# Where the first tile is turned, and where the scatters sit: a gated cross-attention and expert kernel on one core

## Chip, core and metric

One NeuronCore of one Trainium2 chip. The metric is the device time of one execution in microseconds (us). Engine names in the profile: PE is TensorE, PEld its weight loads, DVE VectorE, ACT ScalarE, POOL GpSimd, SP the engine whose queue (SPq) issues most DMAs.

## The reference, cut to what matters

```python
# 16 batches of 128 tokens, width 128; ctx of width 256; 8 heads of 16
x = x + tanh(g_xattn) * xattn(ctx, layernorm(x), mask, mask, ...)
#   k, v from ctx; q from layernorm(x); masked softmax; out = W_out [tgt, update] + b_out
x = x + tanh(g_ffn) * ffn(layernorm(x))
def ffn(x):                                    # 2048 tokens, 9 experts, hidden 352
    scores = sigmoid(x @ gate.T + bias)
    top_scores, selected = top_k(scores, 2)    # normalised to sum 1
    for e in range(9):
        h = silu(x @ w1[e].T) * (x @ w3[e].T)
        out += cw[:, e:e+1] * (h @ w2[e].T)
```

Each token goes to two experts. The kernel writes every token's normalised row twice into a table in HBM (`x_rows`), ordered by expert, and works through that table in 40 tiles of 128 rows. A tile holds the rows of one expert only.

## The kernel before, in words

Every engine runs its own instruction list in the order of the program; semaphores tie the lists together. An engine that waits for a semaphore holds up all that is behind it in its list.

**Projections** (the first 33 us) make keys, queries and values of all batches.

**Attention steps.** `turns(step)` runs step k = 0 to 16 on all engines. In step k, batch k gets its scores (PE), maxima (DVE, L850) and exponentials (ACT, L412); batch k-1 is transposed and multiplied with the values; batch k-2 is turned back, divided (DVE `unturn`, `upd`, L860), multiplied with W_out (PE `gate_and_out`, L1304) and added to x (DVE `second`, L890 to L896, which also takes mean and variance); batch k-3 is normalised (DVE `norm2`, L869, into `stage`), turned (PE `turn_rows`, L1294) and gated (L1302). The 1/sqrt of the variance is taken on POOL: `rstd2_of(b)` (L586 `ve`, L588 `rs`). `norm2(b)` waits for it, and `turn_rows` waits for `norm2`. So in step k the chain is: `second(k-3)` in step k-1, POOL `rstd2_of(k-3)`, DVE `norm2(k-3)`, PE `turn_rows(k)`.

**Routing.** Batches go in four groups of four. When a group's gate logits are there, DVE clamps them, takes the sigmoid (with exponentials from ACT), finds the top two (`find_top`), marks them (`mark_top`), PE ranks them (`rank`, L1257 to L1261), and DVE works out weights and target rows (`weigh`, `keep_ranks`, `place_rows`, `label_rows` with L844). The labels of group g = 0 and 1 are ready at the end of steps 8 and 12, those of group 2 at the end of step 16.

**Scatters.** POOL writes the rows with indirect DMAs (`scatter`, L616), two per batch. Groups 0 and 1 together are 16 pieces, `piece(0)` to `piece(15)`; pieces 0 to 7 are group 0, pieces 8 to 15 group 1. `ROWS` says which piece is issued in which step: a tuple for early (behind `rstd2_of`) and one for late (behind `keep`, the copy of the normalised row). `scatter` of group g first waits for `label_set` g+1. Group 2 is scattered behind the attention steps, group 3 behind the result of tile 1.

**Tables.** `table_counts(n)` (= `count_tiles` and `pass_tiles`) and `table_rows(n)` on DVE work out which rows and which expert each tile has: n = 0 for tiles 0 to 7, n = 1 for 8 to 15, n = 2 for the rest. `table_used` says what is consumed. The loads of tiles 0 to 7 (SP, L319) wait for the landing of all scatters of groups 0 and 1; those of tiles 8 to 15 for group 2's; the rest for group 3's.

**Tiles.** `tile_turns(tile, between)` runs step k = 0 to 42; I call them tile steps. In tile step k PE turns tile k (L1353), makes the two hidden products of tile k-1 (`hidden`, L1342 to L1344, six matmuls), the output of tile k-3 (L1384) and the transposes of tile k-2 (L1393), in this order. ACT splits off the high part of the turned tile (L466), takes the Silu (L473) and copies; DVE makes the low part (`xg_low`, L1066), the product of the gates (`hid`, L1074) and casts an id (L1023). POOL scatters each result to `y_rows` (L643).

The last batch's and last group's chain is laid into the first tile steps: `gate_and_out(17)`, `second(15)`, `norm2(15)`, `turn_rows(18)`, `gate_and_out(18)`, then the routing of group 3. One tile step, `SWITCH`, is special: ACT there loads the table of Exp and that of Silu again (L495, L497), and DVE does ACT's three copies of that step in its place (L1029, L1034, L1039).

At the end PE adds up the last two tiles with one-hot matrices (L1430), the sums come back from `y_rows`, and the output is stored.

Of the kernel before, what the change touches and what calls it, by code (L numbers as in the profile page):

```python
# [59 lines left out]
SWITCH = 3  # L60
VALUES = {0: (0,), 1: (1,), 2: (2,), 3: (3,), 4: (4, 5), 5: (6, 7), 6: (8, 9), 7: (10, 11, 12), 8: (13, 14, 15)}
ROWS = {9: ((0,), (1,)), 10: ((2,), (3,)), 11: ((4,), (5,)), 12: ((6,), (7,)), 13: ((8,), (9,)), 14: ((10,), (11,)), 15: ((12,), (13,)), 16: ((14, 15), ())}
# [8 lines left out]
def build(nc, x, ctxT, mask, first, consts, row_consts, w_srcT, w_tgtT, w_outT, w13T, w2T, gateT, x_rows, y_rows, out):  # L71
    with ExitStack() as ctx:
# [163 lines left out]
        def has(k, lag):  # L236

            return 0 <= k - lag < NT
# [109 lines left out]
        def _(act):  # L348
# [109 lines left out]
            nc.scalar.preload_act_table(ACT.Silu)  # L458
            turned_back(NB + 1)

            def tile(k, r, i):
                if has(k, 0) and not in_switch(k):
                    act.wait_ge(x_turned, k + 1)
                    if k >= 2:
                        act.wait_ge(h3_mm, k - 1)
                    nc.scalar.copy(xg_high[:, r % 2, :], bank[6][:, 0:P]).then_inc(x_high, 1)  # L466
# [197 lines left out]
        def _(dve):  # L664
# [332 lines left out]
            table_used(0)  # L997
            table_counts(1)
# [42 lines left out]
            def within(k):  # L1041

                if k == SWITCH:
                    table_rows(1)
                    result_in_switch(k - 3)
                    turned_in_switch(k - 2)
                    add_one(NG - 1)
                if k == 4:
                    above_knee(NG - 1)
                if k == 5:  # L1050
                    mark_top(NG - 1)
                if k == 6:
                    keep_ranks(NG - 1)
                    place_rows(NG - 1)
                    label_rows(NG - 1)
                if k == 9:
                    table_rows(2)
# [31 lines left out]
            def between(k):  # L1089

                if k == 0:
                    second(NB - 1)
                if k == 1:
                    norm2(NB - 1)
                if k == SWITCH - 1:
                    logits_of(NG - 1)
                    clamp(NG - 1)
                if k == 4:
                    find_top(NG - 1)
                if k == 5:  # L1100
                    weigh(NG - 1)
                if k == 6:
                    table_used(1)
                if k == 7:
                    count_tiles(2)
                if k == 8:
                    pass_tiles(2)
# [25 lines left out]
        def _(pe):  # L1133
# [162 lines left out]

            def gate_and_out(k):

                pe.wait_ge(ul_copied, k - 1)
                if on(k, 3):  # L1300
                    at = 3 * P + (k - 3) % UN * NE
                    nc.tensor.matmul(ps_b[:, at:at + NE], ulT[:, k % 2, 1, :], gate_w[:], start=True, stop=True).then_inc(lg_mm, 1)  # L1302
                if on(k, 2):
                    nc.tensor.matmul(ps_b[:, 2 * P:3 * P], ulT[:, k % 2, 0, :], w_outg[:, 1, :], start=True, stop=True).then_inc(o_mm, 1)  # L1304
# [11 lines left out]
            keep_busy(0, 5)  # L1316
            turn_rows(NB + 1)
# [30 lines left out]
            def tile(k, r, i):  # L1348
                if has(k, 0):
                    pe.wait_ge(ld_tile[r], i * 16 + 16)  # L1350
                    if k >= 1:
                        pe.wait_ge(x_low, k)
                    nc.tensor.transpose(bank[6][:, 0:P], xg[:, r, 0:D], ident).then_inc(x_turned, 1)  # L1353
                if in_switch(k):
                    gate_and_out(NB + 2)
                if has(k, 1):
# [6 lines left out]
                    hidden(bank[2 + q], q, e, 1).then_inc(h3_mm, 1)  # L1363
                if has(k, 0):
# [36 lines left out]
            def between(k):  # L1401

                if k == 0:
                    gate_and_out(NB + 1)
                if k == 5:
                    rank(NG - 1)
# [99 lines left out]
```

## Time and profile before

| what | value |
|---|---|
| median of 3 runs | 213.8 us (213.61 to 214.6) |
| the profiled execution | 213.55 us, of which the span 211.8 us |
| PE, DVE, ACT, POOL busy | 201.5, 146.2, 141.5, 128.3 us |
| granted TensorE clock | 1.00 throughout |
| DMA | 34.91 MB, mean 165 GB/s |

The span runs from the first to the last instruction. In a timeline row the columns are: start and length in us, engine, line, operation, tiles written and read, count, and in brackets how long the engine had been idle and what released it. Starts are more telling than lengths, since the pipelined engines overlap successive instructions.

### The profile page before, as it was taken

The page shows a single profiled execution, that of the slowest core. Times are in us where ns is not written, and L with a number is a line of the kernel's source. Part 1 is how long each engine was busy: PE and PEld are TensorE (multiplying, and loading weights), DVE is VectorE, ACT ScalarE, POOL GpSimd, SP SyncE. Part 2 cuts the span into 40 slices and gives each one's busy share as a digit, 9 for nine tenths or more (in the row PEclk, how much of TensorE's full clock was granted, in tenths as well). Part 3 has the DMA queues.
Part 4 walks back from the last instruction along what each step waited for, and adds up shares of the span by engine and source line. Part 5 has one row for each costly group of instructions (what it writes and reads, how often), then busy time and mean ns, then how long its engine had stood idle before and what let it go on. Part 6 is the DMA issues. An engine that isn't in the chain of part 4 may idle for free.

```text
span 211.8 us, 5793 instructions
## 1 busy us (share of the span) xinstructions
PE 201.5 (95%) x1608; PEld 162.7 (77%) x1608; DVE 146.2 (69%) x523; ACT 141.5 (67%) x398; POOL 128.3 (61%) x231
## 2 busy tenths in 40 slices
PE   8999998999999999999979899999999999999993
PEld 3686575567666676666648789999999999999893
DVE  0369979787889968899987997544343434456674
ACT  2365896999886788588846766766667676666200
POOL 5227655027664686567767867788888856567200
PEclk9999999999999999999999999999999999999999
DMA  5999999999993011000015923422322222270196
GB/s 144 379 365 264 390 408 406 393 392 324 329 354 101 7 35 39 27 26 27 28 52 107 256 64 99 83 85 69 87 69 70 58 62 53 63 246 29 37 346 223
DMA packets 23601, 34.91 MB, mean 165 GB/s; under 512 B 2561, under 2 KB 15878, under 8 KB 23442
## 3 DMA queue, kind: packets, MB, share of 16 engines
q1 hardware_dynamic: 20610, 29.27, 42.6%
q0 software_dynamic: 2240, 4.23, 6.2%
q10 hardware_dynamic: 720, 1.02, 1.6%
q8 instruction: 15, 0.25, 0.5%
q14 instruction: 16, 0.13, 0.2%
HBM read 15.85 MB, written 19.06 MB: 165 GB/s over the span
## 4 chain that ended last, share of the span: by engine, by line
PE 65%; DVE 15%; ACT 5%; issue 5%; DMA 4%; POOL 4%; SPq 1%; POOLq 0%; DVEq 0%; ACTq 0%
PE pt_ps L1384 10%; PE score_ps L1342 5%; PE pt_ps L1393 5%; PE score_ps L1197 5%; PE score_ps L1344 5%; PE score_ps L1343 5%; PE pt_ps L1235 4%; PE ps_a L1247 3%; PE pt_ps L1137 3%; DMA kheads<-y_rows 3%; PE score_ps L1147 3%; DVE less L850 2%; ACT probs L412 2%; PE ps_a L1353 2%; POOL y_rows L643 2%
## 5 line engine op out<-in xcount | busy, mean ns | idle before, releaser
L643 POOL DMA_INDIRECT y_rows<-vals,ids x38 | 37.7, 992 | 14.2 <-ACT vals L484 7.9
L412 ACT ACTIVATE probs<-score_ps,less 128x128 f32<-128x128 f32 x128 | 37.5, 406 | 1.7 <-DVE less L850 1.7
L616 POOL DMA_INDIRECT x_rows<-stage,slot x32 | 32.6, 1018 | 9.1 <-issue 7.7
L1384 PE MATMUL pt_ps<-w,probsT 128*128 x234 | 32.6, 275 | 0.9 <-DVE probsT L1039 0.6
L1384 PEld LDWEIGHTS pt_ps<-w,probsT 128*128 128x128 f32 x234 | 30.8, 191 | 1.6 <-issue 1.4
L1066 DVE TENSOR_TENSOR xg_low<-ps_a,xg_high 128x128 fp32r<-128x128 f32 x40 | 11.6, 290 | 29.2 <-ACT xg_high L466 28.8
L484 ACT ACTIVATE vals<-pt_ps,xg 128x128 f32<-128x128 f32 x38 | 13.9, 367 | 26.6 <-PE pt_ps L1384 26.6
L1342 PE MATMUL score_ps<-w_high,xg_low 128*128 x80 | 29.2, 364 | 0.0
L1344 PE MATMUL score_ps<-w_high,xg_high 128*128 x80 | 25.9, 323 | 0.0
L1343 PE MATMUL score_ps<-w_low,xg_high 128*128 x80 | 25.6, 320 | 0.0
L1074 DVE TENSOR_TENSOR probs<-probs,score_ps 128x352 f32<-128x352 f32 x40 | 20.8, 520 | 6.1 <-ACT probs L473 2.7
L850 DVE TENSOR_REDUCE less<-score_ps 128x4 f32<-128x512 f32 x32 | 21.7, 684 | 3.5 <-PE score_ps L1204 3.4
L473 ACT ACTIVATE probs<-score_ps 128x352 f32<-128x352 f32 x40 | 18.6, 464 | 1.3 <-PE score_ps L1344 1.2
L1393 PE MATMUL pt_ps<-fst,probs 128*128 128x128 f32 x117 | 19.2, 273 | 0.1
L491 ACT COPY probsT<-pt_ps 128x384 f32<-128x384 f32 x38 | 18.2, 478 | 0.3 <-PE pt_ps L1393 0.2
L1197 PE MATMUL score_ps<-kheads,qT 64*128 64x256 f32 x128 | 18.2, 402 | 0.2
L1235 PE MATMUL pt_ps<-fst,probs 128*128 128x128 f32 x128 | 17.1, 274 | 1.0 <-ACT probs L412 1.0
L586 POOL TENSOR_SCALAR ve<-mv 128x1 f32<-128x1 f32 x16 | 3.6, 227 | 20.3 <-DVE mv L896 20.3
L1235 PEld LDWEIGHTS pt_ps<-fst,probs 128*128 128x128 f32 x128 | 14.4, 141 | 2.0 <-ACT probs L412 1.9
L1342 PEld LDWEIGHTS score_ps<-w_high,xg_low 128*128 128x128 f32 x80 | 15.1, 189 | 0.5 <-issue 0.2
L1343 PEld LDWEIGHTS score_ps<-w_low,xg_high 128*128 128x128 f32 x80 | 15.2, 190 | 0.0
L1344 PEld LDWEIGHTS score_ps<-w_high,xg_high 128*128 128x128 f32 x80 | 15.0, 188 | 0.0
(184 smaller groups left out, 442.8 us busy)
## 6 DMA issues: line engine op xcount, KB each, us to landing
x_rows<-pads SPq DMA_DIRECT2D x1, 9945.0 KB, 37.7
w_low<-in_w13T SPq DMA_DIRECT2D x3, 1056.0 KB, 11.5
xg<-x_rows SPq DMA_DIRECT2D x40, 65.0 KB, 2.0
ctx_r<-in_ctxT SPq DMA_DIRECT2D x4, 512.0 KB, 7.5
y_rows<-pads SPq DMA_DIRECT2D x1, 2048.0 KB, 18.7
w<-in_w2T SPq DMA_DIRECT2D x1, 1728.0 KB, 13.2
kheads<-y_rows SPq DMA_DIRECT2D x3, 512.0 KB, 5.0
mask_b<-in_mask SPq DMA_DIRECT2D x4, 256.0 KB, 8.2
```

Of the source, the lines that this page charges most:

```text
L412: last = nc.scalar.activation(probs[:, r % 2, h, :], score_ps[:, r % 2, h, :], ACT.Exp, bias=less[:, r % 2, h:h + 1])
L616: pool.indirect_dma_start(x_rows[:, :], bass.IndirectOffsetOnAxis(ap=slot[:, par, c, p:p + 1], axis=0), stage[:, par, c, p, :], None, boun ...
L643: pool.indirect_dma_start(y_rows[:, :], bass.IndirectOffsetOnAxis(ap=ids[:, s:s + 1], axis=0), yt[:, s, :], None, bounds_check=last_row, o ...
L850: nc.vector.tensor_reduce(less[:, r % 2, here], score_ps[:, r % 2, here, :], AX.X, ALU.max, negate=True).then_inc(lessened, 1)
L1074: nc.vector.tensor_tensor(hid[:, q, :], gated[:, q, :], bank[2 + q][:, 0:HID], ALU.mult).then_inc(hid_done, 1)
L1197: nc.tensor.matmul(score_ps[:, r % 2, half * HH + 2 * pair:half * HH + 2 * pair + 2, :], qT[rows, k * P:(k + 1) * P], kheads[rows, heads, ...
L1235: last = nc.tensor.transpose(pt_ps[:, half, h, :], probs[:, q, half * UN + h, :], ident)
L1342: nc.tensor.matmul(dst[:, 0:HID], xg_low[:, q, :], of(w13_high), start=True, stop=False)
L1343: nc.tensor.matmul(dst[:, 0:HID], xg_high[:, q, :], of(w13_low), start=False, stop=False)
L1344: return nc.tensor.matmul(dst[:, 0:HID], xg_high[:, q, :], of(w13_high), start=False, stop=True)
L1384: last = nc.tensor.matmul(into[:, 0:D], hidT[:, q3, c, :], w2[:, bass.ds(e3, 1), c, :].rearrange("p o d -> p (o d)"), start=(c == 0), stop ...
L1393: last = nc.tensor.transpose(bank[4][:, c * P:(c + 1) * P], hid[:, q2, c0:c0 + P], ident)
```

## The change

What it does, by engine:

- PE: tile 0 is turned behind the filler matmuls (`keep_busy(0, 5)`) and ahead of `turn_rows(17)`; `gate_and_out(17)` moves from behind tile step 0 into tile step 1, behind `hidden` of tile 0; `turn_rows(18)` and `gate_and_out(18)` come one tile step later; so does `rank(3)`.
- ACT: the high part of tile 0 is taken ahead of `turned_back(17)`.
- `SWITCH` goes from 3 to 4, and with it the Exp and Silu tables and the switched copies.
- DVE: `table_used(0)` and `table_counts(1)` leave the place ahead of tile 0. `table_used(0)` goes to tile step 0, `count_tiles(1)` to 2, `pass_tiles(1)` to 3; `table_rows(1)` stays in the switch step and goes behind the two switched copies. `second(15)` moves from behind tile step 0 to inside tile step 1 (ahead of `hid`), `norm2(15)` one step later, all of group 3's routing one step later, `add_one` out of the switch step.
- POOL: `piece(2)` is issued in step 9 rather than 10, and so every second piece a place sooner: step 9 has three pieces, step 16 one. `piece(8)`, the first of group 1, goes from early in step 13 to late in step 12, and `piece(15)` from second to first in step 16.

```diff
-SWITCH = 3
+SWITCH = 4
-ROWS = {9: ((0,), (1,)), 10: ((2,), (3,)), 11: ((4,), (5,)), 12: ((6,), (7,)), 13: ((8,), (9,)), 14: ((10,), (11,)), 15: ((12,), (13,)), 16: ((14, 15), ())}
+ROWS = {9: ((0,), (1, 2)), 10: ((3,), (4,)), 11: ((5,), (6,)), 12: ((7,), (8,)), 13: ((9,), (10,)), 14: ((11,), (12,)), 15: ((13,), (14,)), 16: ((15,), ())}
@@ scalar
+            def high_rows(k, r):
+                act.wait_ge(x_turned, k + 1)
+                if k >= 2:
+                    act.wait_ge(h3_mm, k - 1)
+                nc.scalar.copy(xg_high[:, r % 2, :], bank[6][:, 0:P]).then_inc(x_high, 1)
+            high_rows(0, 0)
             turned_back(NB + 1)
             def tile(k, r, i):
-                if has(k, 0) and not in_switch(k):
+                if has(k, 0) and k >= 1 and not in_switch(k):
+                    high_rows(k, r)
@@ vector
             norm2(NB - 2)
-            table_used(0)
-            table_counts(1)
             def within(k):
+                if k == 0:
+                    table_used(0)
+                if k == 1:
+                    second(NB - 1)
+                if k == 2:
+                    count_tiles(1)
+                if k == SWITCH - 1:
+                    pass_tiles(1)
                 if k == SWITCH:
-                    table_rows(1)
                     result_in_switch(k - 3)
                     turned_in_switch(k - 2)
+                    table_rows(1)
+                if k == 5:
                     add_one(NG - 1)
-                if k == 4:
                     above_knee(NG - 1)
-                if k == 5:
+                if k == 6:
                     mark_top(NG - 1)
...
             def between(k):
-                if k == 0:
-                    second(NB - 1)
-                if k == 1:
+                if k == 2:
                     norm2(NB - 1)
...
@@ tensor
+            def turn_tile(k, r, i):
+                pe.wait_ge(ld_tile[r], i * 16 + 16)
+                if k >= 1:
+                    pe.wait_ge(x_low, k)
+                nc.tensor.transpose(bank[6][:, 0:P], xg[:, r, 0:D], ident).then_inc(x_turned, 1)
             keep_busy(0, 5)
+            turn_tile(0, 0, 0)
             turn_rows(NB + 1)
             def tile(k, r, i):
...
                     hidden(bank[2 + q], q, e, 1).then_inc(h3_mm, 1)
+                if k == 1:
+                    gate_and_out(NB + 1)
             def between(k):
-                if k == 0:
-                    gate_and_out(NB + 1)
-                if k == 5:
+                if k == 6:
                     rank(NG - 1)
```

Left out are the remaining steps of the routing in `within` and `between`, all one tile step later (`keep_ranks` to `label_rows` 7, `table_rows(2)` 10, `find_top` 5, `weigh` 6, `table_used(1)` 7, `count_tiles(2)` 8, `pass_tiles(2)` 9).

## Rows read from the trace of the kernel before

**Rows 1.** The page: busy time of the engines, and the last chain's shares.

```profile
PE 201.5 (95%) x1608; PEld 162.7 (77%) x1608; DVE 146.2 (69%) x523; ACT 141.5 (67%) x398; POOL 128.3 (61%) x231
...
PE 65%; DVE 15%; ACT 5%; issue 5%; DMA 4%; POOL 4%; SPq 1%; POOLq 0%; DVEq 0%; ACTq 0%
```

**Rows 2.** Stretches: length, busy time of each engine, clock, DMA share, GB/s.

```profile
110.00:137.00 27.00, 25.14 (x183) 23.14 (x184) 21.74 (x105) 17.36 (x45) 20.61 (x29) 1.00 0.50 123
137.00:197.00 60.00, 59.67 (x464) 59.44 (x463) 28.36 (x93) 39.91 (x116) 45.33 (x91) 1.00 0.29 80
```

**Rows 3.** Timeline of POOL: steps 9 and 10, and the scatters of group 3.

```profile
74.58 0.98 POOL L616 DMA_INDIRECT x_rows<-stage,slot  x1 [0.17 <-issue]
75.59 0.24 POOL L586 TENSOR_SCALAR ve<-mv 128x1 f32<-128x1 f32 x1
75.92 0.57 POOL L588 TENSOR_TENSOR rs<-ve,minus_half 128x1 f32<-128x1 f32 x1
...
126.24 0.99 POOL L616 DMA_INDIRECT x_rows<-stage,slot  x1 [1.43 <-DVE slot L844]
127.54 0.97 POOL L616 DMA_INDIRECT x_rows<-stage,slot  x1 [0.30 <-issue]
```

**Rows 4.** Timeline of DVE: `norm2` of step 10, labels of group 1, `norm2` of step 13.

```profile
76.82 0.34 DVE L869 SCALAR_TENSOR_TENSOR stage<-xs,mv,rs 128x128 f32<-128x128 f32 x1
...
90.52 0.20 DVE L844 CAST slot<-slot_f 128x8 int32<-128x8 f32 x1
...
91.67 0.34 DVE L869 SCALAR_TENSOR_TENSOR stage<-xs,mv,rs 128x128 f32<-128x128 f32 x1
```

**Rows 5.** Timeline of PE: the turned row of steps 10 and 13.

```profile
77.22 0.33 PE L1294 MATMUL ps_b<-fst,stage 128*128 128x128 f32 x1
...
92.07 0.33 PE L1294 MATMUL ps_b<-fst,stage 128*128 128x128 f32 x1
```

**Rows 6.** Timeline of POOL: pieces 14 and 15 in step 16.

```profile
104.67 1.09 POOL L616 DMA_INDIRECT x_rows<-stage,slot  x1 [0.19 <-issue]
106.07 0.97 POOL L616 DMA_INDIRECT x_rows<-stage,slot  x1 [0.30 <-issue]
```

**Rows 7.** Timeline of PE: fillers, tile 0, `gate_and_out(17)`, `hidden`, tiles 6 to 8.

```profile
108.37 1.24 PE L1267 MATMUL score_ps<-ones 128*128 128x512 bf16 x5
...
110.88 0.33 PE L1353 MATMUL ps_a<-fst,xg 128*128 128x128 f32 x1 [0.61 <-DMA xg<-x_rows]
...
111.19 0.47 PE L1304 MATMUL ps_b<-w_outg,ulT 128*128 128x128 f32 x2
...
112.24 0.42 PE L1342 MATMUL score_ps<-w_high,xg_low 128*128 x1
...
113.37 0.42 PE L1342 MATMUL score_ps<-w_high,xg_low 128*128 x1
...
123.53 0.31 PE L1353 MATMUL ps_a<-fst,xg 128*128 128x128 f32 x1
...
125.83 0.27 PE L1353 MATMUL ps_a<-fst,xg 128*128 128x128 f32 x1
...
127.89 0.27 PE L1353 MATMUL ps_a<-fst,xg 128*128 128x128 f32 x1
```

**Rows 8.** Timeline of DVE: `count_tiles(1)`, `xg_low` 0, `second(15)`, `hid` 0, `mark_top(3)`.

```profile
110.18 0.16 DVE L955 TENSOR_SCALAR in_tiles<-placed 1x9 f32<-1x9 f32 x1
...
111.62 0.29 DVE L1066 TENSOR_TENSOR xg_low<-ps_a,xg_high 128x128 fp32r<-128x128 f32 x1
111.83 0.28 DVE L890 TENSOR_TENSOR xs<-ps_b,xs 128x128 f32<-128x128 f32 x1
...
113.57 0.52 DVE L1074 TENSOR_TENSOR probs<-probs,score_ps 128x352 f32<-128x352 f32 x1 [0.58 <-ACT probs L473]
...
122.79 0.22 DVE L799 TENSOR_TENSOR choices<-cst,top_at 128x72 f32<-128x72 f32 x1
```

**Rows 9.** Timeline of POOL: the result scatter of tile 24.

```profile
170.33 0.99 POOL L643 DMA_INDIRECT y_rows<-vals,ids  x1 [0.60 <-POOL ids L633]
```

More of the change, by code:

```diff
@@ L458, in _ @@
             nc.scalar.preload_act_table(ACT.Silu)
+            def high_rows(k, r):
[4 more added lines that the diff above has]
+            high_rows(0, 0)
             turned_back(NB + 1)
             def tile(k, r, i):
-                if has(k, 0) and not in_switch(k):
[L463 to L466, printed above, removed]
+                if has(k, 0) and k >= 1 and not in_switch(k):
+                    high_rows(k, r)
                 if has(k, 1):
@@ L1041, in within @@
             def within(k):
+                if k == 0:
[6 more added lines that the diff above has]
+                    pass_tiles(1)
                 if k == SWITCH:
-                    table_rows(1)
                     result_in_switch(k - 3)
                     turned_in_switch(k - 2)
+                    table_rows(1)
+                if k == 5:
                     add_one(NG - 1)
-                if k == 4:
                     above_knee(NG - 1)
-                if k == 5:
+                if k == 6:
                     mark_top(NG - 1)
-                if k == 6:
+                if k == 7:
                     keep_ranks(NG - 1)
@@ L1055, in within @@
                     label_rows(NG - 1)
-                if k == 9:
+                if k == 10:
                     table_rows(2)
@@ L1097, in between @@
                     clamp(NG - 1)
-                if k == 4:
+                if k == 5:
                     find_top(NG - 1)
-                if k == 5:
+                if k == 6:
                     weigh(NG - 1)
-                if k == 6:
+                if k == 7:
                     table_used(1)
-                if k == 7:
+                if k == 8:
                     count_tiles(2)
-                if k == 8:
+                if k == 9:
                     pass_tiles(2)
@@ L1348, in tile @@
             def tile(k, r, i):
[L1349 to L1353, printed above, removed]
+                if has(k, 0) and k >= 1:
+                    turn_tile(k, r, i)
                 if in_switch(k):
@@ L1401, in between @@
             def between(k):
-                if k == 0:
-                    gate_and_out(NB + 1)
-                if k == 5:
+                if k == 6:
                     rank(NG - 1)
```

## The prediction

> **What bounds the kernel now.** I read the page first: PE is busy 95% of the span and carries 65% of the chain that ended last, DVE 15%, POOL only 4% [rows 1]. The small shares matter, because the stretches differ. From 137 to 197 us PE is busy 59.67 of 60 us: nothing but PE's own work sets the pace there, and tile follows tile every 2.06 us (125.83 to 127.89) [rows 2, 7]. From 110 to 137 it is busy 25.14 of 27 us while DVE is busy 21.74 and POOL 20.61 [rows 2]: here PE waits, mostly for DVE. The change touches this junction, and through POOL the attention steps 9 to 16. So the questions are: when does PE reach tile 7 or 8 at full pace, and does a POOL instruction of an attention step come on the path. I then went through the timelines of POOL, DVE and PE.
>
> **POOL, step 9: one more scatter.** POOL works in order. In step 9 the late scatter starts at 74.58 and takes 0.98; `ve` of step 10 starts at 75.59, right at its end, and `rs` ends at 75.92 + 0.57 = 76.49 [rows 3]. DVE's `norm2` started at 76.82, so 0.33 was to spare, of which 0.03 is the release [rows 4]. Now two late scatters stand there. The second costs a gap of 0.30 and 0.98, as in the pair at 126.24 and 127.54 (1.30 from start to start) [rows 3]: 1.28. `rs` ends at 77.77, `norm2` starts at 77.80, 0.98 late; PE's L1294, 0.40 behind `norm2` before (77.22) [rows 5], comes 0.98 late. All of PE's step is behind it in its list, ACT's exponentials are behind the copy of what it turns, and the second maxima behind `norm2` on DVE. PE is the longest of the three in these steps, so nothing gives the time back. Bounds: 0 (a scatter that holds nothing up) and 1.3 (all of it on the path); the rows lie at 0.98, and I take that.
>
> The Trainium skill speaks against this. "DMA: Bandwidth & Descriptors", section "Anatomy of one DMA — SWDGE (gpsimd) path", counts descriptor generation as small and says that many descriptors can be emitted before the added cost shows. The trace disagrees for this indirect form: 0.98 us, with the next POOL instruction right at the end. By the rule this term would be 0, and the next one would lose 0.98; that is a rival below.
>
> **POOL, step 12: piece 8 waits for labels.** Piece 8 belongs to group 1, whose labels DVE finishes at 90.52 + 0.20 = 90.72, at the very end of its step 12 [rows 4]. Before, it was issued in step 13, behind `rstd2_of(10)`. Now it stands late in step 12 and POOL stops on it, with `rstd2_of(10)` queued behind. It starts some 0.28 after the label (the released one at 126.24 shows a wait of this kind) [rows 3], at 91.00, ends at 91.98; `ve` and `rs` take 0.90 (75.59 to 76.49), to 92.88; `norm2(10)` starts at 92.91, not 91.67 [rows 4]. PE's L1294 of step 13 follows at 93.31, not 92.07 [rows 5]: 1.24 late, and again all is behind it. It had no slack at all: `norm2` began when `upd` left DVE. Bounds: 0, if POOL could pass the waiting scatter, and 1.4 with the longest scatter, 1.09 [rows 6]; I take 1.24. In the other steps each piece only changes its name, not its place in time, and costs 0.
>
> **POOL, step 16: piece 15 lands sooner.** From its start (106.07) to PE's turn of tile 0 (110.88, released by the load) it took 4.81 us [rows 6, 7]. It now starts at 104.67 and is 0.12 longer: tile 0 is ready at 109.60. SP has nothing else ahead of these loads. The fillers end at 108.37 + 1.24 = 109.61 [rows 7], so the turn at 109.63 waits for nothing and costs PE nothing, since `turn_rows(17)` behind it waits for `norm2(14)` till 109.9 anyway. If the landing were later, `turn_rows(17)` would be late by as much.
>
> **The junction on PE and DVE.** (Times of the clock before; 2.22 are to be added.) From the turn of tile 0 to `hidden` of it the chain took 112.24 - 110.88 = 1.36 [rows 7]. From 109.63 that gives 110.99: a lead of 1.25. What is next late is `hid` 0 on DVE. `second(15)` stands ahead of it and needs `gate_and_out(17)`, now behind the six matmuls of `hidden` (1.06 of the 1.13 from 112.24 to 113.37), so W_out's product starts at 110.99 + 1.06 + 0.24 and takes 0.47 [rows 7]: 112.76. The add starts at about 112.8, and the three instructions of `second` take 0.86 with their waits; `hid` 0 starts at 113.6 or so. Before it started at 113.57 [rows 8]. The lead has gone into DVE's waiting: DVE has only `table_used(0)` (0.38) to do meanwhile, where before it did the table counts.
>
> From `hid` 0 to `mark_top(3)` DVE took 122.79 - 113.57 = 9.22 [rows 8], nearly without a pause. To it come `count_tiles(1)` and `pass_tiles(1)`, which stood ahead of tile 0: 111.62 - 110.18 = 1.44 [rows 8], and the DVE work of one tile more (0.21 + 0.44 + 0.06 = 0.71, from start to start), and about 0.1 for waits on the gate logits and on the output in the switch step: 11.5. `mark_top(3)` starts at about 125.05. PE's `rank(3)` is released by it and now stands ahead of tile 7, not of tile 6. Before, the turn behind it came 123.53 - 122.79 = 0.74 behind `mark_top` [rows 7, 8], so tile 7 is turned at 125.79 against 125.83, and tile 8, by the 2.30 of that step, at 128.09 against 127.89 [rows 7]: 0.20 late. From there all is as before. Putting `table_rows(1)` behind the switched copies saves PE a wait at the output matmuls, but the DVE work stays, and it ends in the wait at `rank`. Bounds of this term: -2.9, if PE never waited from tile 1 to tile 7 (its own work there is 12.1 us by the spacing of its rows, from 110.8 on), and +1.3, if each moved item waits once more; the rows that decide are DVE's, so I take +0.20.
>
> **The end.** Labels of group 3 come about 2.3 later, relative to this clock, so POOL's eight scatters and behind them the result scatters start 2.3 late, 2.1 against PE. At tile 24 POOL had just caught up: that scatter waited 0.60 for its own id, not for a result [rows 9]. Its own spacing there is 0.99 + 0.03 + 0.20 + 0.60 = 1.82 against PE's 2.06, so 2.1 us of arrears take 9 tiles, till tile 33 of 38. It is just hidden: 0.
>
> **The sum.** 0.98 + 1.24 + 0.20 = 2.42. The profiled execution took 213.55 us (span 211.8), the changed one 215.97; the median of the runs shown is 213.8, 0.25 above the profiled one, so I forecast 216.2, 1.1% slower.
>
> **The rivals.**
> - *The lead is kept.* DVE's waits turn out shorter and PE keeps the 1.25 at tile 7, with both POOL delays: 213.8 + 2.22 - 1.25 = 214.8. For it: DVE has pauses in the early tile steps into which work may fit. Against: the 11.5 us of DVE work ahead of `rank`.
> - *Cheap scatters* (the skill's rule): posting takes POOL next to nothing. Step 9 costs 0, step 12 only the wait, 1.24 - 0.98 = 0.26, the junction 0.20: 214.3. Against: [rows 3].
> - *The other side, faster: the junction's waits go.* The lead and the copies ahead of `table_rows(1)` take out every wait of PE up to tile 7: -2.9, against +2.22: 213.1; below that if a POOL delay is smaller. Its place is `rank(3)`, and it decides if `mark_top(3)` starts before PE is ready for it, about 122.2 on the clock before. Against: DVE would have to do 11.5 us of work in 8.6.
> - *The end shows.* If POOL's arrears are a microsecond larger than I reckon, or DVE's late one-hot rows slow POOL, the last result scatter, and the sum behind it, come up to 1 us later: 217.2. For it: tile 24 without slack [rows 9].
>
> **How the numbers follow.** Forecast 0.55, lead kept 0.13, cheap scatters 0.08, faster side 0.10, the end 0.14. The forecast alone has 215.4 to 216.9. The range goes from 214.0, which takes in the cheap scatters and the kept lead, to 217.8 with the end; the faster side and a tenth of the rest lie outside. About 0.5% (1.07 us) is what a measurement can tell from no change: slower beyond it are forecast and end, 0.69; within it the two middle cases, 0.21; faster 0.10.
>
> **What would show it.** In the changed profile: L616 late in step 12 with an idle time of about 3 us released by DVE `slot`; L1294 of steps 10 and 13 each released by `stage`, with PE idle about 1 us; the turn of tile 0 right behind the fillers; `hid` 0 no sooner behind the fillers than now; PE idle about 1 us ahead of `rank`; `y_rows` scatters waiting for ACT again at the end. I am wrong if POOL's `ve` starts before the scatter ahead of it has ended, or if tile 8 is turned less than 19 us behind the fillers' start (before: 19.5).

## The result, and the profile after

| | before | after |
|---|---|---|
| median (runs) | 213.87 us (4) | 217.22 us (4; 216.65 to 217.65) |
| ratio after/before, 95% interval | | 1.0143 (1.0115 to 1.0171) |
| profiled execution, span | 213.55, 211.8 | 217.65, 215.9 |

The change makes the kernel slower: by 3.35 us between the medians, by 1.4% in the ratio on record. The forecast was 216.2 with a range up to 217.8: the sign, both POOL delays and the range hold; the sum is 1.0 too small.

**A common clock first.** The spans differ by 4.1, not 3.3. The rest is older than the change: the row of batch 5 that PE turns in step 8, ahead of every edit, stands 0.76 later in the profiled execution of after. That is the start-up: in the fourteen kernels of this document, which are the same up to there, the row stands anywhere from 67.86 to 69.26. So all marks below are counted from the start of that row. First before, then after, PE's timeline:

```profile
68.12 0.27 PE L1294 MATMUL ps_b<-fst,stage 128*128 128x128 f32 x1
```

```profile
68.88 0.27 PE L1304 MATMUL ps_b<-fst,stage 128*128 128x128 f32 x1
```

| mark, us from that row | before | after | later by | forecast |
|---|---|---|---|---|
| `turn_rows(17)` on PE | 41.82 | 44.09 | 2.27 | 2.22 |
| tile 0 turned | 42.76 | 43.61 | 0.85 | 0.97 |
| `hid` 0 starts on DVE | 45.45 | 47.59 | 2.14 | 2.25 |
| `mark_top(3)` starts on DVE | 54.67 | 60.12 | 5.45 | 4.48 |
| tile 7 turned | 57.71 | 60.84 | 3.13 | 2.18 |
| tile 8 turned | 59.77 | 63.24 | 3.47 | 2.42 |
| tile 13 turned | 70.31 | 73.60 | 3.29 | 2.42 |

(The forecast's times of the clock before, plus the 2.22.) All is as forecast down to `hid` 0, and the microsecond is lost between there and `mark_top(3)`.

The page of after (line numbers have moved: L1304 was L1294, L622 was L616, L592 and L594 were L586 and L588). POOL's share of the chain has risen from 4% to 7%, PE's has fallen from 65% to 62% [rows 1]; the scatter group says whom POOL waits for:

```profile
PE 202.2 (94%) x1608; PEld 163.1 (76%) x1608; DVE 146.4 (68%) x523; ACT 141.7 (66%) x398; POOL 128.7 (60%) x231
...
PE 62%; DVE 15%; POOL 7%; issue 5%; ACT 5%; DMA 4%; SPq 1%; POOLq 0%; ACTq 0%; DVEq 0%
...
L622 POOL DMA_INDIRECT x_rows<-stage,slot x32 | 32.9, 1027 | 14.5 <-DVE slot L850 7.3
```

Stretches of after, columns as in [rows 2], laid 3 us later. The tiles' stretch is PE's alone as before; at the junction PE is busy 23.89 of 27 us where it was 25.14 [rows 2]:

```profile
113.00:140.00 27.00, 23.89 (x174) 22.01 (x175) 21.34 (x105) 16.30 (x42) 18.09 (x25) 1.00 0.42 107
140.00:199.00 59.00, 59.00 (x459) 58.98 (x459) 27.32 (x92) 39.68 (x115) 46.62 (x92) 1.00 0.30 84
```

**The two POOL delays.** POOL's timeline of after, steps 9 and 10, then 12 and 13:

```profile
75.34 0.98 POOL L622 DMA_INDIRECT x_rows<-stage,slot  x1 [0.17 <-issue]
76.63 0.97 POOL L622 DMA_INDIRECT x_rows<-stage,slot  x1 [0.30 <-issue]
77.62 0.25 POOL L592 TENSOR_SCALAR ve<-mv 128x1 f32<-128x1 f32 x1
...
92.66 0.98 POOL L622 DMA_INDIRECT x_rows<-stage,slot  x1 [3.59 <-DVE slot L850]
93.66 0.25 POOL L592 TENSOR_SCALAR ve<-mv 128x1 f32<-128x1 f32 x1
```

In step 9 the second late scatter starts 1.29 behind the first, and `ve` stands right at its end. In step 12 piece 8 stops POOL for 3.59 us on the labels (3 forecast), with `ve` and `rs` of batch 10 behind it, which `norm2(10)` needs. PE's timeline shows what follows, where both rows had no idle time ahead of them before [rows 5]:

```profile
78.97 0.33 PE L1304 MATMUL ps_b<-fst,stage 128*128 128x128 f32 x1 [0.91 <-DVE stage L875]
...
95.00 0.33 PE L1304 MATMUL ps_b<-fst,stage 128*128 128x128 f32 x1 [1.21 <-DVE stage L875]
```

From row to row step 10 grows from 4.30 to 5.29 (+0.99; forecast 0.98), step 13 from 4.43 to 5.68 (+1.25; forecast 1.24). Step 14 grows by 0.11 and step 11 gives 0.07 back; neither was in the sum.

**The junction.** PE's timeline of after, answering to [rows 7]: tile 0 right behind the fillers, the W_out product of batch 15 behind the six of `hidden` 0, row 18, tiles 6, 7 and 8:

```profile
111.42 1.24 PE L1277 MATMUL score_ps<-ones 128*128 128x512 bf16 x5
112.49 0.27 PE L1312 MATMUL ps_a<-fst,xg 128*128 128x128 f32 x1
...
114.01 0.42 PE L1360 MATMUL score_ps<-w_high,xg_low 128*128 x1
...
115.21 0.47 PE L1321 MATMUL ps_b<-w_outg,ulT 128*128 128x128 f32 x2
...
119.26 0.30 PE L1304 MATMUL ps_b<-fst,stage 128*128 128x128 f32 x1 [0.34 <-issue]
...
125.40 0.55 PE L1410 MATMUL pt_ps<-fst,probs 128*128 128x128 f32 x3 [0.72 <-DVE probs L1086]
125.78 0.27 PE L1312 MATMUL ps_a<-fst,xg 128*128 128x128 f32 x1
...
129.51 0.19 PE L1267 MATMUL ps_b<-both,rows_below 128*128 128x36 bf16 x1 [1.13 <-DVE both L811]
...
129.72 0.31 PE L1312 MATMUL ps_a<-fst,xg 128*128 128x128 f32 x1
...
132.12 0.27 PE L1312 MATMUL ps_a<-fst,xg 128*128 128x128 f32 x1
```

DVE's timeline of after, answering to [rows 8]: `second(15)`, `hid` 0, the gate logits, the first copy of the switch step, `over` of the routing, `mark_top(3)`:

```profile
115.71 0.29 DVE L896 TENSOR_TENSOR xs<-ps_b,xs 128x128 f32<-128x128 f32 x1 [0.89 <-PE ps_b L1321]
...
116.47 0.50 DVE L1086 TENSOR_TENSOR probs<-probs,score_ps 128x352 f32<-128x352 f32 x1
...
120.91 0.20 DVE L881 TENSOR_TENSOR z<-ps_b,cst 128x36 f32<-128x36 f32 x1 [0.84 <-PE ps_b L1319]
...
122.65 0.35 DVE L1038 TENSOR_SCALAR vals<-pt_ps,xg 128x128 f32<-128x128 f32 x1 [0.59 <-PE pt_ps L1401]
...
126.25 0.67 DVE L783 TENSOR_SCALAR over<-sigs 128x36 f32<-128x36 f32 x1
...
129.00 0.22 DVE L805 TENSOR_TENSOR choices<-cst,top_at 128x72 f32<-128x72 f32 x1
```

PE stands 1.13 us ahead of `rank(3)`, as forecast; but it also lost 0.72 a step earlier to DVE's `hid`. From `hid` 0 to `mark_top(3)` DVE took 129.00 - 116.47 = 12.53 us, not 11.5. It stood still for the gate logits (0.84) and for the output (0.59), 1.43 together; before, these two instructions waited 0.24 and nothing. And L783 took 0.67 instead of 0.35. I had put 0.1 for all of this. Two instructions went the other way: from start to start `key` (L770, before L764) took 0.21 instead of 0.42, and the cast of the packed experts (L987, before L981) 0.10 instead of 0.27, together 0.38 less.

### The profile page after: what moved, and what is told of

It reads as the page before. It is cut to its first block, busy times and chain, and to the rows that moved or that the text cites. A ratio compares the mean times of both kernels' runs of the same rounds, so it can differ in the third digit from the quotient of the medians.

```text
span 215.9 us, 5792 instructions
## 1 busy us (share of the span) xinstructions
PE 202.2 (94%) x1608; PEld 163.1 (76%) x1608; DVE 146.4 (68%) x523; ACT 141.7 (66%) x398; POOL 128.7 (60%) x231
## 3 DMA queue, kind: packets, MB, share of 16 engines
q10 hardware_dynamic: 720, 1.02, 1.6%
## 4 chain that ended last, share of the span: by engine, by line
PE 62%; DVE 15%; POOL 7%; issue 5%; ACT 5%; DMA 4%; SPq 1%; POOLq 0%; ACTq 0%; DVEq 0%
PE pt_ps L1401 10%; PE score_ps L1360 5%; PE score_ps L1362 5%; PE score_ps L1361 5%; PE pt_ps L1410 5%; PE score_ps L1207 4%; PE pt_ps L1147 4%; PE pt_ps L1245 3%; DMA kheads<-y_rows 3%; PE ps_a L1257 3%; PE score_ps L1157 2%; ACT probs L412 2%; DVE less L856 2%; PE ps_a L1312 2%; POOL y_rows L649 2%
## 5 line engine op out<-in xcount | busy, mean ns | idle before, releaser
L622 POOL DMA_INDIRECT x_rows<-stage,slot x32 | 32.9, 1027 | 14.5 <-DVE slot L850 7.3
L1245 PEld LDWEIGHTS pt_ps<-fst,probs 128*128 128x128 f32 x128 | 14.4, 141 | 2.0 <-ACT probs L412 1.9
L592 POOL TENSOR_SCALAR ve<-mv 128x1 f32<-128x1 f32 x16 | 3.7, 229 | 20.0 <-DVE mv L902 20.0
L1410 PEld LDWEIGHTS pt_ps<-fst,probs 128*128 128x128 f32 x117 | 14.0, 141 | 1.5 <-DVE probs L1086 1.5
```

Of the source, the lines that this page charges most:

```text
L622: pool.indirect_dma_start(x_rows[:, :], bass.IndirectOffsetOnAxis(ap=slot[:, par, c, p:p + 1], axis=0), stage[:, par, c, p, :], None, boun ...
L1245: last = nc.tensor.transpose(pt_ps[:, half, h, :], probs[:, q, half * UN + h, :], ident)
L1410: last = nc.tensor.transpose(bank[4][:, c * P:(c + 1) * P], hid[:, q2, c0:c0 + P], ident)
```

## The experiments

What was open: whether the two delays are caused by the pieces' places alone, and which edit of the tile phase costs the rest. `ROWS` of before, of after, and three others. PE marks as above, "later" against before; "step 10" and "step 13" are the change of the distance between two turned rows:

| kernel | ratio to before (95%) | step 10 | step 13 | `turn_rows(17)` later | tile 13 later |
|---|---|---|---|---|---|
| after | 1.0143 (1.0115-1.0171) | +0.99 | +1.25 | 2.27 | 3.29 |
| before_new_scatters | 1.0135 (1.009-1.018) | +0.99 | +1.26 | 2.31 | 2.24 |
| only_step9 | 1.0062 (1.004-1.0084) | +0.99 | 0.00 | 0.93 | 0.90 |
| only_step12 | 1.0111 (1.007-1.0152) | 0.00 | +1.25 | 1.38 | 1.35 |
| after_old_scatters | 1.0054 (1.0032-1.0076) | 0.00 | 0.00 | 0.98 | 1.35 |
| after_scatters13 | 1.0056 (1.0034-1.0077) | +0.01 | 0.00 | 0.10 | 1.08 |
| row18_ahead_of_unpack | 1.0072 (1.0045-1.0099) | +0.01 | 0.00 | 0.10 | 1.41 |
| second_back | 1.0001 (0.9986-1.0017) | 0.00 | 0.00 | 0.09 | 0.03 |
| early_tile_alone | 1.0004 (0.9986-1.0022) | +0.01 | +0.01 | 0.12 | -0.22 |
| before_scatters13 | 0.9997 (0.9979-1.0015) | -0.01 | +0.01 | 0.10 | 0.11 |
| unpack_sooner | 1.0011 (0.9994-1.0029) | 0.00 | 0.00 | 0.12 | 0.50 |
| routing_later | 0.9958 (0.9943-0.9974) | 0.00 | 0.00 | 0.10 | -0.91 |
| routing_later_copies_first | 0.9952 (0.9933-0.9971) | 0.00 | +0.01 | 0.09 | -0.78 |

The marks are one execution each, but steady: where two kernels share their code up to a mark, it agreed to 0.1 us. The times carry the start-up too, half a microsecond and more either way. Before was measured beside each set of kernels: its median was 214.31 beside before_new_scatters, only_step9, only_step12 and after_old_scatters, 214.02 beside after_scatters13, row18_ahead_of_unpack, second_back and early_tile_alone, and 213.95 beside the last four. The ratios are those on record and not quotients of these medians; for routing_later the medians alone would give 0.9978.

### Undo the parts

**before_new_scatters**: before, with `ROWS` of after.

```diff
-ROWS = {9: ((0,), (1,)), 10: ((2,), (3,)), ... 12: ((6,), (7,)), ... 16: ((14, 15), ())}
+ROWS = {9: ((0,), (1, 2)), 10: ((3,), (4,)), ... 12: ((7,), (8,)), ... 16: ((15,), ())}
```

> The kernel before with the changed list ROWS alone. Theory (the two POOL delays are 2.2 of the 3.3 us): the delays come whole, 0.98 in step 10 and 1.18 in step 13, and the sooner load of tile 0 gives nothing, since the table counts hold up its low part: 213.9 + 2.2 = 216.1. Rival (scatters cost POOL next to nothing, and the whole loss sits in the tile phase): 213.9. Rival (tile 0's sooner load pays by itself, up to 0.6): 215.5.

216.60 us. The scatters' places alone give both delays, and 2.24 of the 3.29. Up to row 17 the kernel before, with these places, loses what after loses (2.31 and 2.27), so nothing of that part comes from the edits of the tile phase.

**only_step9**: before, with one scatter more in step 9 and none late in step 12.

```diff
-ROWS = {9: ((0,), (1,)), 10: ((2,), (3,)), 11: ((4,), (5,)), 12: ((6,), (7,)), ...
+ROWS = {9: ((0,), (1, 2)), 10: ((3,), (4,)), 11: ((5,), (6,)), 12: ((7,), ()), ...
```

> The kernel before with a third scatter in step 9, pieces 3 to 7 one place sooner, none late in step 12, and pieces 8 to 15 where they were. Theory: 0.98 us from the scatter ahead of the 1/sqrt of step 10, so 214.9; in the trace PE waits about 0.9 for the normalised row of step 10 and not in step 13. Rival (cheap scatters): 213.9.

215.56 us. POOL and PE:

```profile
75.69 0.99 POOL L616 DMA_INDIRECT x_rows<-stage,slot  x1 [0.17 <-issue]
76.99 0.97 POOL L616 DMA_INDIRECT x_rows<-stage,slot  x1 [0.30 <-issue]
77.97 0.26 POOL L586 TENSOR_SCALAR ve<-mv 128x1 f32<-128x1 f32 x1
```

```profile
79.33 0.33 PE L1294 MATMUL ps_b<-fst,stage 128*128 128x128 f32 x1 [0.91 <-DVE stage L869]
```

One scatter, once, costs 0.99 us on PE, and at tile 13 0.90 of it is still there. The rival of the cheap scatters (nothing in step 9) falls: the Trainium skill's "DMA: Bandwidth & Descriptors", section "Anatomy of one DMA — SWDGE (gpsimd) path", counts descriptor generation as small, but here a scatter of 128 rows keeps POOL busy, 0.97 to 0.99 us in these rows, and POOL's next instruction starts right at its end.

**only_step12**: before, with piece 8 late in step 12, and the pieces of steps 9 to 11 in their old places.

```diff
-... 12: ((6,), (7,)), 13: ((8,), (9,)), 14: ((10,), (11,)), 15: ((12,), (13,)), 16: ((14, 15), ())}
+... 12: ((6,), (7, 8)), 13: ((9,), (10,)), 14: ((11,), (12,)), 15: ((13,), (14,)), 16: ((15,), ())}
```

> The kernel before with piece 8 late in step 12 behind piece 7, the pieces behind it a place sooner, steps 9 to 11 as they were. Theory: POOL stops on the labels of group 1, and 1.2 us come on the path in step 13: 215.1; the wait in the trace is shorter than in the changed kernel, since piece 7 stands ahead of it, but it ends at the same label. Rival (a waiting scatter can be passed, or the time is made good in steps 14 to 16): 213.9 to 214.2.

216.41 us, 2.1 above the before beside it, where the trace has 1.35 at tile 13. These are six executions, from 215.63 to 217.51, and the trace is of one at the lower end (215.70); what made the longer ones longer is in no trace. POOL waits from 89.6 for the labels, and `ve` is behind:

```profile
91.76 0.98 POOL L616 DMA_INDIRECT x_rows<-stage,slot  x1 [2.15 <-DVE slot L844]
92.75 0.26 POOL L586 TENSOR_SCALAR ve<-mv 128x1 f32<-128x1 f32 x1
```

```profile
94.10 0.33 PE L1294 MATMUL ps_b<-fst,stage 128*128 128x128 f32 x1 [1.21 <-DVE stage L869]
```

The wait is 2.15 here and 3.59 in after, and the delay is 1.25 in both. How long POOL waits is not the price; the price is when it goes on, and that is set by the labels. In the traces the two parts add up: 0.90 + 1.35 = 2.25 against 2.24.

**after_old_scatters**: after, with `ROWS` of before (the diff of before_new_scatters the other way round).

> The changed kernel with the list ROWS of before. Theory: both delays go, -2.2, but the load of tile 0 lands 1.3 later, and PE stands on it ahead of the last attention row's transposes: +1.0 to +1.4, in all 216.0 to 216.4. Rival (the whole loss sits in the tile phase): 217.2 or more. Rival (the late load is hidden by DVE's waits): 215.0.

215.55 us, under the 216.0 to 216.4 that I expected. Both delays are gone, and another one has come: with pieces 14 and 15 both in step 16, tile 0 lands late, and PE stands on it with the last attention row behind. PE's timeline:

```profile
111.19 0.33 PE L1312 MATMUL ps_a<-fst,xg 128*128 128x128 f32 x1 [1.01 <-DMA xg<-x_rows]
111.35 0.27 PE L1298 MATMUL ps_b<-fst,upd 128*128 128x128 f32 x1
```

So the early turn needs the sooner scatters. Row 17 is 0.98 late, tile 13 1.35; the tile phase adds 0.37 here, not 1.02, and that is where my expectation was too high.

**after_scatters13**: after, with the extra scatter in step 13, a step in which labels are there and POOL has room.

```diff
+... 12: ((6,), (7,)), 13: ((8,), (9, 10)), 14: ((11,), (12,)), 15: ((13,), (14,)), 16: ((15,), ())}
```

> The changed kernel, but the extra scatter is taken up late in step 13 (pieces 9 and 10) rather than in step 9, so that piece 8 stays where its labels are ready and piece 15 is still first in step 16. Theory: both POOL delays go (step 14 had 0.17 of slack and loses under 0.1), tile 0's load stays early, and what is left is the tile phase: 1.0 over the kernel before from the row transposed in step 17 to tile 13, so 214.9 to 215.1 beside a before of 213.9. Rival (the tile phase costs the 0.20 that was forecast): 214.2. Rival (step 13 is no better a place): 216.0.

214.98 us. Piece 15 is as early as in after, step 14 is 0.10 longer, and no other step moves. What stays is nearly the tile phase alone: +1.08 at tile 13, of which 0.98 arises behind row 17. It is the base for the next three.

### What costs the microsecond in the tile phase

**row18_ahead_of_unpack**: `turn_rows(18)`, whose gate product DVE's `z` waits for, moved ahead of the register load of the next experts (`unpack_next`: PE reads the numbers of the next four tiles' experts, packed in one word by DVE, into a register).

```diff
                 if k == 1:
                     gate_and_out(NB + 1)
+                if k == SWITCH - 1:
+                    turn_rows(NB + 2)
                 if has(k, 0):
                     if r % PACK == PACK - 1:
...
-                if k == SWITCH - 1:
-                    turn_rows(NB + 2)
```

> after_scatters13 with turn_rows(18) on PE ahead of the register load of the next four experts, not behind it. In the changed kernel's trace that load runs from 118.1 to 119.0 and the transpose starts at 119.26, though the normalised row was there at 118.49. Theory (the exposed register load starts DVE's wait on the gate logits, and with it 0.4 to 0.6 of the tile phase's 1.0): 0.4 to 0.6 faster than after_scatters13; DVE's wait ahead of z falls from 0.84 to about 0.3. Rival (the load only moves to the output matmuls behind, and the chain over DVE is the same): equal to after_scatters13 within 0.1 in the trace.

A miss: 215.26 us, tile 13 at 1.41, 0.33 worse than its base. DVE's wait for the gate logits grew from 0.84 to 1.19 instead of going, and PE lost 0.71 ahead of the output matmuls. First DVE, then PE:

```profile
118.49 0.20 DVE L881 TENSOR_TENSOR z<-ps_b,cst 128x36 f32<-128x36 f32 x1 [1.19 <-PE ps_b L1319]
```

```profile
115.98 0.27 PE L1304 MATMUL ps_b<-fst,stage 128*128 128x128 f32 x1
116.97 0.93 PE L1401 MATMUL pt_ps<-w,probsT 128*128 x6 [0.71 <-issue]
```

The row did come sooner, but its gate product stands one tile step further on (L1319), behind the output. The load only changed its place: bare in front of the output matmuls, it delays both.

**unpack_sooner**: after_scatters13, with that register load one tile step sooner.

```diff
+                    if k == 2:
+                        unpack_next(0, 1)
-                    if r % PACK == PACK - 1:
+                    if r % PACK == PACK - 1 and k != 3:
```

> after_scatters13 with the register load of experts 4 to 7 in tile step 2, behind hidden of tile 1, where PE waits for hid 0 anyway, rather than in step 3. Theory (that load takes 0.95 in the changed place and is bare there, 0.4 ahead of turn_rows(18) or, in row18_ahead_of_unpack, 0.7 ahead of the output matmuls): the wait ahead of turn_rows(18) goes, and tile 8 is turned 0.3 to 0.5 sooner than in after_scatters13 (61.01 from the row of step 8). Rival (DVE's path from hid 0 to mark_top does not hang on it): 61.0.

214.18 us, tile 13 at 0.50: 0.58 regained, a little more than I expected. PE's register loads (count, shortest, median and longest in ns, first and last start) of before, after and this kernel:

```profile
L1328 PEldq TENSOR_LOAD <-experts_packed x2: 310/402/495, 110.0 to 115.8; - x2
```

```profile
L1346 PEldq TENSOR_LOAD <-experts_packed x2: 492/717/942, 113.1 to 118.1; - x2
```

```profile
L1346 PEldq TENSOR_LOAD <-experts_packed x2: 397/446/494, 110.5 to 113.0; - x2
```

The load in tile step 3 takes 0.94 us in after; a step sooner it takes under 0.5, and the wait for the gate logits falls from 0.84 to 0.22:

```profile
117.76 0.20 DVE L881 TENSOR_TENSOR z<-ps_b,cst 128x36 f32<-128x36 f32 x1 [0.22 <-PE ps_b L1319]
```

From `hid` 0 to `mark_top(3)` it is 0.75 less than in the base. The waits are 0.63 less; L783 (0.30 here, 0.67 there) gives another 0.36, and other instructions take 0.24 more.

The traces also say when this load is long, and they say it of more kernels than the three above. It took 0.89 to 0.98 us in nine of the fourteen kernels, and in all nine the DMA engines were full while it ran (DMA share 1.01 to 1.10); it took 0.31 to 0.47 in the other five, with a share of 0.21 to 0.76. The stretch of the load in after, and that in before (length, busy times, clock, DMA share, GB/s, as in [rows 2]):

```profile
118.07:119.01 0.94, 0.85 (x6) 0.56 (x4) 0.91 (x6) 0.65 (x3) 0.75 (x1) 1.00 1.10 297
```

```profile
115.78:116.09 0.31, 0.31 (x4) 0.31 (x3) 0.31 (x2) 0.31 (x1) 0.31 (x1) 1.00 0.21 17
```

No run changes the DMA traffic alone, so the two go together in fourteen kernels, and that one causes the other is not shown. Nor is the share the whole story: the load of tiles 0 to 3 took 0.49 to 0.50 in all kernels, at shares of 0.35 to 0.56. Nor does a long load cost time by itself: in before_scatters13 it took 0.97, PE stood 0.38 us ahead of the output matmuls, and tile 13 came 0.11 late. What it costs depends on what stands behind it.

**second_back**: after_scatters13, with `gate_and_out(17)` and `second(15)` back in `between(0)`, ahead of `hidden` 0, as before the change.

```diff
             def between(k):
+                if k == 0:
+                    gate_and_out(NB + 1)        # and on DVE: second(NB - 1)
...
-                if k == 1:
-                    gate_and_out(NB + 1)
```

> after_scatters13 with gate_and_out(17) and second(15) back behind tile step 0, ahead of the turn of tile 1. Theory (the lead of tile 0 was spent in DVE's two waits of 0.9 ahead of second(15), and the product of W_out fits where PE waits for the low part of tile 0): hid 0 starts 0.5 to 0.8 sooner, and mark_top(3) and tile 8 by 0.4 to 0.8. Rival (the six matmuls of hidden come as much later as the add comes sooner): equal to after_scatters13.

214.00 us, tile 13 at +0.03: all of the 1.08 is gone. DVE and PE:

```profile
111.50 0.29 DVE L896 TENSOR_TENSOR xs<-ps_b,xs 128x128 f32<-128x128 f32 x1 [0.93 <-PE ps_b L1321]
...
116.90 0.20 DVE L881 TENSOR_TENSOR z<-ps_b,cst 128x36 f32<-128x36 f32 x1
...
118.62 0.35 DVE L1038 TENSOR_SCALAR vals<-pt_ps,xg 128x128 f32<-128x128 f32 x1 [0.58 <-PE pt_ps L1399]
```

```profile
L1346 PEldq TENSOR_LOAD <-experts_packed x2: 323/408/493, 110.0 to 114.5; - x2
```

`second(15)` is not without a wait (0.93), but the wait now stands at 111, where DVE has time, and `hid` 0 starts 0.82 sooner than in its base (44.59 against 45.41). The wait for the logits is gone, and the register load, unmoved in the list, starts 0.4 sooner and is short (0.32). So undoing the order of `second(15)` and `hidden` 0 is enough to take the whole 1.05 back. Most of it comes by the sooner `hid` 0; from `hid` 0 to `mark_top(3)` only 0.25 is gained (12.26 against 12.51). The forecast had the late `hid` 0 in it, so it is unpack_sooner, more than this run, that speaks to what the forecast missed, and the 0.58 and the 1.05 are not parts of one sum. The wait for the output (0.58) is still here: it is in every kernel that has the switched copies ahead of `table_rows(1)`, and in none of the others. Nor does the order always cost as much: after_old_scatters has it too, but the load took 0.47 there, DVE's `z` waited 0.35, and `mark_top(3)` came 11.77 behind `hid` 0, not 12.53.

### What an early tile 0 is worth

**early_tile_alone**: before with the `ROWS` of after_scatters13, tile 0 turned ahead of row 17 (and on ACT its high part taken ahead of `turned_back(17)`), and the table counts spread over tile steps 0 to 2; the chain of the last batch and group not moved, `SWITCH` 3.

```diff
             keep_busy(0, 5)
+            turn_tile(0, 0, 0)
             turn_rows(NB + 1)
...
-            table_used(0)
-            table_counts(1)
...
+                if k == 0:
+                    table_used(0)
+                if k == 1:
+                    count_tiles(1)
+                if k == SWITCH - 1:
+                    pass_tiles(1)
```

> The kernel before with the scatters as in after_scatters13, tile 0 turned and its high part taken ahead of row 17, and the table counts spread (used 0, counts 1, pass 2), but the chain of the last batch, the switch and the routing where they were. Theory (the loss of the tile phase comes from the routing a tile later with more DVE work ahead of rank, not from tile 0): tile 8 is turned 0.3 to 0.8 sooner than in the kernel before, 213.2 to 213.7 beside 213.9. Rival (DVE has the same work ahead of rank, and it sets the end): 213.9. Rival (spread counts cost as such): 214.5 and more.

Mostly a miss: 214.17 us, no difference. Tile 0 is 1.30 sooner, `mark_top(3)` 0.18 and tile 13 0.22. The lead is eaten by DVE, whose work up to `mark_top` has not become less.

**before_scatters13**: before with the `ROWS` of after_scatters13, nothing else.

> The kernel before with the scatters of after_scatters13 alone. It tells what the sooner load of tile 0 is worth by itself. Theory (nothing: the table counts on DVE hold the low part of tile 0 till 111.6): from the row transposed in step 8 to the turn of tile 13 the kernel before takes 70.31, and this one 70.3 to 70.4, 0.1 being step 14's; 213.9 to 214.0. Rival (the load is on the path): up to 0.6 less.

213.90 us, tile 13 at +0.11. Having tile 0's rows sooner is worth nothing where the turn stays behind row 17, and the extra scatter in step 13 is nearly free.

**routing_later**: early_tile_alone, with the routing of group 3 from `find_top` on one tile step later.

```diff
-                if k == 4:
+                if k == 5:
                     find_top(NG - 1)
-                if k == 5:
+                if k == 6:
                     mark_top(NG - 1)         # and on PE: rank(NG - 1)
```

With them move `weigh` (to 6), `keep_ranks` to `label_rows` and `table_used(1)` (7), `count_tiles(2)` (8), `pass_tiles(2)` (9) and `table_rows(2)` (10), as in the change.

> early_tile_alone (SWITCH 3, second(15) where it was) with find_top and all routing behind it one tile step later, as in the changed kernel. Theory (DVE's work per tile step falls under PE's 2.06 in steps 4 and 5 and rank no longer stands on it): tile 8 turned 0.5 to 1.2 sooner than in early_tile_alone (59.57), about 213.0. Rival (the routing a step later is itself what costs, as one more tile's DVE work ahead of rank): 60.0 and more, 214.4.

213.48 us against 213.95, ratio 0.9958 (0.9943 to 0.9974): faster than before, by some 0.4%. PE's timeline: it now comes to `rank` with DVE ready, no wait ahead of it.

```profile
123.94 0.27 PE L1312 MATMUL ps_a<-fst,xg 128*128 128x128 f32 x1
...
126.00 0.18 PE L1267 MATMUL ps_b<-both,rows_below 128*128 128x36 bf16 x1
...
126.20 0.31 PE L1312 MATMUL ps_a<-fst,xg 128*128 128x128 f32 x1
```

This is the place at which my rival on the other side decides (`mark_top(3)` ready before PE is), reached by asking for it one tile later. Tile 13 is 0.91 sooner than before the change: of the lead of 1.3 at tile 0 some 0.7 more has come through than in early_tile_alone.

**routing_later_copies_first**: the same, with the two copies of the switch step ahead of `table_rows(1)`, as in the change.

```diff
                 if k == SWITCH:
-                    table_rows(1)
                     result_in_switch(k - 3)
                     turned_in_switch(k - 2)
-                    add_one(NG - 1)
+                    table_rows(1)
                 if k == 4:
+                    add_one(NG - 1)
                     above_knee(NG - 1)
```

> routing_later with the two switched copies ahead of table_rows(1), and add_one in step 4. It leaves of the changed kernel only the later switch and the later chain of the last batch out. Theory: PE's wait for the copied hidden (about 1 us in step 4) shrinks, but hid 2 comes later by the table's 1.5, so within 0.3 of routing_later either way. Rival (the order in the switch step is what made the changed kernel slow): 0.8 or more slower than routing_later.

212.94 us, ratio 0.9952 (0.9933 to 0.9971); tile 13 0.13 later than without. The intervals of the two overlap, and time and mark point opposite ways: this edit is worth nothing that these runs can tell. Both beat before and after, by 0.4 to 0.5% against before.

This kernel also answers a question that I had not put. It differs from second_back in one thing: `SWITCH` is 3 and not 4, and the chain that goes with it (`count_tiles(1)`, `pass_tiles(1)`, `norm2(15)`, `turn_rows(18)`, `gate_and_out(18)`, the copies, `add_one`) stands one tile step sooner. That is worth 0.81 us at tile 13 (-0.78 against +0.03) and shows in the times (0.9952 against 1.0001, intervals apart). So the tile phase of the change holds two losses over what the early tile and the later routing can give: 0.81 by the later switch step and its chain, and 1.05 by the later `second(15)`; -0.78 + 0.81 + 1.05 = 1.08, the base.

## Why the prediction was right, and what of it was not

- **Step 9, +0.98: right.** 0.99 in after and in only_step9. The 0.33 to spare ahead of `norm2` was real, and all behind it went on the path.
- **Step 12, +1.24: right.** 1.25 in after and in only_step12, whatever the length of the wait.
- **Nothing else in the attention steps: nearly.** Step 14 is 0.11 longer, step 11 is 0.07 shorter.
- **Tile 0 turned right behind the fillers, and `hid` 0 no sooner: right.** In after_scatters13, where the attention steps hardly move, tile 0 is turned 1.32 sooner and `hid` 0 starts at 45.41 against 45.45.
- **The junction, +0.20: the mis-sized term; it measured 1.02** (3.29 - 2.27). The mechanism was the one told (`second(15)` behind `hidden` 0, DVE's list too long ahead of `rank`), but the step "about 0.1 for waits on the gate logits and on the output" failed. They took 1.43 where before they took 0.24, and one instruction 0.32 more than before. With the added work (1.44 and 0.71), and less the 0.38 of the two shorter instructions, these make 9.22 + 1.44 + 0.71 + 1.19 + 0.32 - 0.38 = 12.50, against the 12.53 of the rows. I had asked what DVE has to do while it waits for `second`, and not what stands ahead of `z` on PE three steps on. The normalised row of batch 15 was there at 118.49, but PE turned it at 119.26, behind its register load (118.07 to 119.01): with the load moved, the 0.84 becomes 0.22 and 0.58 us come back (unpack_sooner). The 0.59 goes with the copies' place ahead of `table_rows(1)`. I had seen that this order saves PE a wait at the output matmuls, and not that it gives DVE one. The 0.32 of L783 was tried by no run.
- **The range of this term, -2.9 to +1.3, held it.** It lay near the upper end that I had named as "if each moved item waits once more", which is about what happened. I took the row of DVE's busy time as the decider, and left the waits in between at nearly nothing.
- **The stated range held by luck.** I had given 215.4 to 216.9 to the forecast alone, and 217.22 lies outside that. It is inside the full range because of the room up to 217.8, which was left for a late end, and the end was not late.
- **The end, 0: right, by too careful a figure.** I had reckoned POOL's own spacing at 1.82, from a row with a wait in it. In after, while it catches up, it is 1.49, and it has caught up at 184.68, where it waits for ACT's result again: that is tile 29, not 33. The last scatter has no arrears. POOL's timeline:

```profile
176.27 0.99 POOL L649 DMA_INDIRECT y_rows<-vals,ids  x1 [0.28 <-POOL ids L639]
...
177.76 0.99 POOL L649 DMA_INDIRECT y_rows<-vals,ids  x1 [0.28 <-POOL ids L639]
...
184.68 0.99 POOL L649 DMA_INDIRECT y_rows<-vals,ids  x1 [0.84 <-ACT vals L490]
...
201.07 0.99 POOL L649 DMA_INDIRECT y_rows<-vals,ids  x1 [0.58 <-POOL ids L639]
```

- **The rivals.** "The end shows" gave 217.2, the time that was measured, for a cause that did not act. "Cheap scatters" fell to only_step9. "The lead is kept" and "the waits go" did not happen in after; with the chain of the last batch left in place and the routing a step later they do in part (routing_later, -0.91).
- My own mark for being wrong, tile 8 under 19 us behind the fillers' start, was not met: 132.12 - 111.42 = 20.7, against 19.5 before.

Left open: whether the full DMA engines make the register load long. They were full in all nine kernels with a long load and in none of the five with a short one, but no run changes the one without the other. Left open too is what makes L783 take 0.67.

## What to carry to other kernels

An indirect scatter is work of the POOL that issues it, here about 1 us, in POOL's order: before moving it, look at what stands behind it in the next step and how much that has to spare, and never put it ahead of its labels while something urgent is queued behind. When a lead is made at the start of a chain, follow it through the engine that carries most of the work; here DVE gave back 1.1 of the 1.3 us until its result was asked for one step later. And a delayed item is to be followed to its users' users: the wait it makes may stand three steps on.

## What the runs showed of the hardware

- A register load of PE from a table on chip (the second one, in tile step 3, or 2 in unpack_sooner) took 0.31 us in before, 0.32 in second_back, 0.40 in unpack_sooner, 0.44 in only_step9 and 0.47 in after_old_scatters, with a DMA share of 0.21 to 0.76 over it. It took 0.89 to 0.98 in the other nine kernels, with a share of 1.01 to 1.10. In after, after_scatters13 and row18_ahead_of_unpack PE stood for 0.34, 0.36 and 0.71 us behind it.
- The 128 x 36 `TENSOR_SCALAR` L783 took 0.66 to 0.67 us in after, after_scatters13 and second_back, where it started 0.34 behind the start of a result scatter of POOL (126.25 and 125.91 in after), and 0.30 in after_old_scatters, unpack_sooner and row18_ahead_of_unpack, where it started just ahead of one or at the end of one. In routing_later_copies_first it started 0.67 behind the start of a scatter and took 0.31. That POOL's scatter is the cause was not tried.
- The start-up, ahead of step 8, varied by up to 1.4 us between the profiled executions of these kernels, while marks behind it agreed to a tenth where the code is the same. Two spans can't be subtracted before that is taken off.
